# Reordering side work in a fused attention, feed-forward and gated-attention kernel on one core

## The reference

```python
def layernorm(x, gamma, beta):
    mean = jnp.mean(x, axis=-1, keepdims=True)
    std = jnp.sqrt(jnp.sum((x - mean) ** 2, axis=-1, keepdims=True) / (d - 1))
    return gamma * (x - mean) / (std + EPS) + beta

h = layernorm(x + multihead(x, x, x, sa_wq, sa_wk, sa_wv, sa_wo, causal=True), ln1_g, ln1_b)
h = layernorm(h + multihead(h, encoding, encoding, ca_wq, ca_wk, ca_wv, ca_wo, causal=False), ln2_g, ln2_b)
ff = jax.nn.relu(h @ ff_w1.T + ff_b1) @ ff_w2.T + ff_b2
x = layernorm(h + ff, ln3_g, ln3_b)
# gated attention, one head; q = x, k = v = context
qp, kp, vp = q @ Wq + bq, k @ Wk + bk, v @ Wv + bv
w = softmax(einsum('bqd,bkd->bqk', qp, kp) / sqrt(256))
y = einsum('bqk,bkd->bqd', w, vp)
gate = jnp.concatenate((qp, y), axis=-1) @ Wg + bg
out = y * mask * sigmoid(gate) + q
```

## Time and profile before

| what | value |
|---|---|
| median of 3 runs | 798.07 us (797.2 to 802.29) |
| the profiled execution | 799.49 us, its span 797.6 us |
| mean granted TensorE clock | 0.985 of full speed |
| PE, PEld busy | 753.8 us (94%), 620.5 us (78%) |
| DVE, ACT, POOL busy | 539.8 (68%), 526.0 (66%), 488.6 us (61%) |
| DMA | 77.05 MB, mean 97 GB/s |

### The profile page before, as it was taken

How to read it: one execution, slowest core, us unless ns; L and a number is a source line. 1 busy time by engine, 2 the same in 40 slices (tenths; PEclk the granted TensorE clock), 3 DMA queues, 4 the chain that set the end, 5 groups by cost and what they waited for, 6 DMA issues and landing times.

```text
span 797.6 us, 19831 instructions
## 1 busy us (share of the span) xinstructions
PE 753.8 (94%) x7136; PEld 620.5 (78%) x7136; DVE 539.8 (68%) x1202; ACT 526.0 (66%) x1241; POOL 488.6 (61%) x606
## 2 busy tenths in 40 slices
PE   6998999999999999788889999999999999999997
PEld 4786778878887776565568889888888879888875
DVE  4435778787887987876877666666666655575575
ACT  5432366566565566566878888888777888757663
POOL 3413377777677677767756666666565578665530
PEclk9998999999999999989989999999999999999999
DMA  9796697788765666435442222222220100012223
GB/s 287 173 278 178 132 148 133 144 133 137 136 123 108 112 108 125 105 86 119 88 83 57 39 57 57 59 56 55 56 47 6 61 2 5 10 51 65 64 79 102
DMA packets 105323, 77.05 MB, mean 97 GB/s; under 512 B 43277, under 2 KB 101983, under 8 KB 104963
## 3 DMA queue, kind: packets, MB, share of 16 engines
q1 hardware_dynamic: 101866, 72.89, 43.1%
q10 hardware_dynamic: 3360, 2.90, 1.2%
HBM read 25.75 MB, written 11.69 MB: 47 GB/s over the span
## 4 chain that ended last, share of the span: by engine, by line
PE 72%; DVE 7%; ACT 5%; issue 4%; POOL 1%; DMA 0%; ACTq 0%; DVEq 0%; POOLq 0%
PE a_misc L89 14%; PE a_pair L89 12%; PE a_s L1060 10%; PE a_pair L846 5%; PE a_s L822 4%; PE a_pair L864 4%; PE a_s L820 4%; PE a_pair L1019 4%; PE a_pair L1003 3%; PE a_pair L1159 3%; PE a_s L980 2%; PE a_s L1118 2%; DVE a_nm L1536 2%; PE a_pair L867 2%; ACT a_pT L1369 1%
## 5 line engine op out<-in xcount | busy, mean ns | idle before, releaser
L1227 ACT ACTIVATE a_pT<-a_pair 128x512 f32<-128x512 f32 x192 | 113.4, 597 | 76.8 <-PE a_pair L846 69.2
L2074 POOL TENSOR_TENSOR c_hidden<-c_hid,c_hidden 128x256 fp32r<-128x256 f32 x128 | 94.8, 741 | 108.4 <-ACT c_hidden L1403 108.2
L1536 DVE TENSOR_REDUCE a_nm<-a_s 128x2 f32<-128x512 f32 (+1 forms) x192 | 127.2, 677 | 50.2 <-PE a_s L822 49.4
L1060 PE MATMUL a_s<-c_w,c_hidden 128*128 128x256 f32 x768 | 117.1, 292 | 0.0
L1369 ACT ACTIVATE a_pT<-a_pair 77x512 f32<-77x512 f32 x128 | 75.1, 589 | 54.1 <-PE a_pair L1003 52.3
L89 PE MATMUL a_pair<-c_fxh,c_w 128*128 128x256 f32 x512 | 100.0, 288 | 1.5 <-ACT c_hid L1395 1.5
L1962 POOL TENSOR_SCALAR_AFFINE_SELECT a_pT<-a_pT 128x256 f32<-128x256 f32 (+1 forms) x192 | 89.2, 485 | 16.1 <-ACT a_pT L1227 16.0
L1060 PEld LDWEIGHTS a_s<-c_w,c_hidden 128*128 128x128 f32 x768 | 98.6, 190 | 0.4 <-issue 0.4
L1700 DVE TENSOR_REDUCE a_nm<-a_s 128x5 f32<-128x385 f32 (+1 forms) x96 | 55.4, 578 | 50.4 <-PE a_s L980 50.1
L89 PEld LDWEIGHTS a_pair<-c_fxh,c_w 128*128 128x128 f32 x512 | 79.3, 191 | 1.7 <-ACT c_hid L1395 1.7
L846 PE MATMUL a_pair<-a_sq,a_sk 98*128 98x256 bf16 (+1 forms) x512 | 75.3, 250 | 4.9 <-ACT a_pT L1227 4.7
(11 more groups left out here) (268 smaller groups left out, 2030.9 us busy)
## 6 DMA issues: line engine op xcount, KB each, us to landing
a_sq<-a_parts SPq DMA_DIRECT2D x96, 128.0 KB, 4.3
a_sk<-a_parts SPq DMA_DIRECT2D x96, 128.0 KB, 4.3
a_sq<-c_parts SPq DMA_DIRECT2D x96, 128.0 KB
x<-in_xT SPq DMA_DIRECT2D x16, 256.0 KB, 5.1
res<-in_x SPq DMA_DIRECT2D x16, 256.0 KB, 5.2
out<-g_fin SPq DMA_DIRECT2D x15, 256.0 KB, 2.1
a_sk<-kc_parts SPq DMA_DIRECT2D x96, 38.5 KB
g_vv<-vv_rows SPq DMA_DIRECT2D x16, 154.0 KB
```

Of the source, the lines that this page charges most:

```text
L1060: last = mt(down[:, qt * D:(qt + 1) * D], (hh, hl)[x](m)[:, qt * P:(qt + 1) * P], w2(y, m), start=m == 0 and qt == 0 and i == 0, stop=m == ...
L1227: nc.scalar.activation(pT[g % NPT][:], stps[g % 2][:], ACT.Exp).then_inc(s_exp, 1)
L1536: nc.vector.tensor_reduce(nm[c % 2][:, QT * heads[0] + qt:QT * heads[-1] + qt + 1:QT], sps[g % 2][:].rearrange("p (h k) -> p h k", h=len(h ...
L2074: nc.gpsimd.tensor_tensor(hl(m), hid[n % NHID][:], f32(hh(m)), ALU.subtract).then_inc(c_hl, 1)
```

## The change

It changes no arithmetic; it moves instructions and changes three semaphore waits.

- The context products use three banks, `kps[0]`, `kps[1]` and `tps[0]` (`key_ps`); product n waits for remainder n-3. `project_qk(0)`, which also writes `tps`, now waits for all six remainders.
- At n = 16 CROSS slot (0, 1) stands behind causal slot 2 instead of 1, so on every engine causal slot (16, 2), with the last causal shift, comes first.
- `first_deviations` of elements 8 to 11 goes from n = 16, slots 2, 5, 7 to n = 17, slots 8, 10, 11, in each ahead of what VectorE did there.
- At n = 15 the residual of element 12 comes ahead of `turn_av` instead of behind.
- Five pieces of feed weights are split one CROSS slot earlier on ScalarE (four on GpSimd).
- `cross_part_three` moves from slot 5, behind `cross_scale`, to slot 4, behind `shifted_rows2`, for every element.
- Group 8 to 11 of the third norm takes steps one and two in slots 4 and 6 of m = 18 instead of slots 2 and 3 of m = 19; step two of element 15 goes from CROSS (22, 6) to the end of GATED (12, 0).
- `normed(e + 3)` moves from GATED slot k = 3 to k = 1, and waits for `g_h` instead of `g_zg`.

```diff
@@ -150,6 +150,7 @@
     kps, tps, fps = [ps(f"k{i}") for i in range(2)], [ps(f"t{i}") for i in range(2)], [t.pair1[:, 512 * i:512 * (i + 1)] for i in range(2)]
     vps, vec = t.misc[:, 0:512], t.misc[:, 512:1024]
     qk_ps = lambda c: tps if c < 2 else kps
+    key_ps = lambda n: (kps + tps[0:1])[n % 3]
 
     w_loaded = {n: sem("xw_" + n) for n in raw}
     small, biases, c_loaded = sem("x_small"), sem("x_biases"), [sem("x_ctx") for _ in range(NC)]
@@ -245,15 +246,15 @@
                     pe.wait_ge(s_wl, 1)
                 if ot == 0:
                     pe.wait_ge(s_ch, c + 1)
-                atleast(pe, s_kr, n - 1)
+                atleast(pe, s_kr, n - 2)
                 for kt in range(KT):
                     for part in range(2):
-                        mt(kps[n % 2][:, 0:cn], cwk[part][:, kt, ot * P:(ot + 1) * P], ch[:, kt, c0:c0 + cn],
+                        mt(key_ps(n)[:, 0:cn], cwk[part][:, kt, ot * P:(ot + 1) * P], ch[:, kt, c0:c0 + cn],
                            start=kt == 0 and part == 0, stop=False, skip_group_check=True)
                 if ot == 0:
                     pe.wait_ge(s_cl, c + 1)
                 for kt in range(KT):
-                    last = mt(kps[n % 2][:, 0:cn], cwk[0][:, kt, ot * P:(ot + 1) * P], cl[:, kt, c0:c0 + cn],
+                    last = mt(key_ps(n)[:, 0:cn], cwk[0][:, kt, ot * P:(ot + 1) * P], cl[:, kt, c0:c0 + cn],
                               start=False, stop=kt == KT - 1, skip_group_check=True)
                 last.then_inc(s_k, 1)
 
@@ -272,6 +273,8 @@
 
             def project_qk(c):
                 pe.wait_ge(t.s_xl, c + 1)
+                if c == 0:
+                    pe.wait_ge(s_kr, KT * NC)
                 if c < 2:
                     atleast(pe, t.s_r1, 2 * c)
                 else:
@@ -364,7 +367,7 @@
                 ot, c = divmod(n, NC)
                 c0, cn = CCH[c]
                 act.wait_ge(s_k, n + 1)
-                nc.scalar.activation(parts[:, 0, c0 // SC:(c0 + cn) // SC, ot, :], byb(kps[n % 2], 0, cn), ACT.Copy).then_inc(s_kp1, 1)
+                nc.scalar.activation(parts[:, 0, c0 // SC:(c0 + cn) // SC, ot, :], byb(key_ps(n), 0, cn), ACT.Copy).then_inc(s_kp1, 1)
                 act.wait_ge(s_kr, n + 1)
                 nc.scalar.activation(parts[:, 1, c0 // SC:(c0 + cn) // SC, ot, :], byb(rest[n % 2], 0, cn), ACT.Copy).then_inc(s_kp2, 1)
                 if n in (2, 3):
@@ -427,7 +430,7 @@
                 c0, cn = CCH[c]
                 dve.wait_ge(s_kp1, n + 1)
                 atleast(dve, s_kp3, n - 1)
-                nc.vector.tensor_tensor(byb(rest[n % 2], 0, cn), byb(kps[n % 2], 0, cn), parts[:, 0, c0 // SC:(c0 + cn) // SC, ot, :],
+                nc.vector.tensor_tensor(byb(rest[n % 2], 0, cn), byb(key_ps(n), 0, cn), parts[:, 0, c0 // SC:(c0 + cn) // SC, ot, :],
                                         ALU.subtract).then_inc(s_kr, 1)
                 if n in (3, 4):
                     weight_low(n - 2)
@@ -579,8 +582,8 @@
     w2 = lambda a, m: w2_parts[a][m // 2][:, m % 2 * D:(m % 2 + 1) * D]
     pieces = [(raw_w[p // 2][:, p % 2], p // 2, w1_parts[0][p][:], w1_parts[1][p][:]) for p in range(4)]
     pieces += [(raw_w[2 + p // 2][:, p % 2], 2 + p // 2, w2_parts[0][p][:], w2_parts[1][p][:]) for p in range(4)]
-    piece_high = {(-1, 2): 0, (-1, 6): 1, (2, 1): 2, (2, 3): 3, (2, 5): 4, (3, 1): 5, (3, 3): 6, (4, 2): 7}
-    piece_low = {(-1, 3): 0, (-1, 7): 1, (2, 2): 2, (2, 4): 3, (2, 6): 4, (3, 2): 5, (3, 4): 6, (4, 3): 7}
+    piece_high = {(-1, 2): 0, (-1, 6): 1, (2, 0): 2, (2, 2): 3, (2, 4): 4, (3, 0): 5, (3, 2): 6, (4, 2): 7}
+    piece_low = {(-1, 3): 0, (-1, 7): 1, (2, 1): 2, (2, 3): 3, (2, 6): 4, (3, 1): 5, (3, 3): 6, (4, 3): 7}
     hid = [at(f"hid{i}", [P, S], F32, "a_o1", 4 * S * i) for i in range(2)] + [at("hid2", [P, S], F32, "a_on1")]
 
     s_ps, st_ps, av_ps, hy, qm, down = sps[0], stps[0], avps[0], bank0, bank1, sps[1]
@@ -652,7 +655,7 @@
     group_of = lambda c: next(i for i, r in enumerate(feed_groups) if c in r)
 
     beside = {B - 4: [-4], B - 3: [-3], B - 2: [-2], B - 1: [-1], B: [0], B + 1: [1], B + 2: [2, 3], B + 3: [4, 5]}
-    late = {B - 3: [0, 3, 6, 9, 11, 11, 11, 11], B: [0, 1, 3, 4, 6, 8, 11, 11],
+    late = {B - 3: [0, 3, 6, 9, 11, 11, 11, 11], B: [0, 2, 3, 4, 6, 8, 11, 11],
             B + 1: [0, 3, 6, 9, 9, 9, 11, 11]}
     order = []
     for n in range(-3, B + 4):
@@ -1439,7 +1442,7 @@
                 if c == 0:
                     stacks_dead(act, 0)
                 act.wait_ge(g_nmr, group_of(c) + 1)
-                atleast(act, g_zg, c - 1)
+                atleast(act, g_h, c - 1)
                 for qt in range(QT):
                     n = QT * c + qt
                     last = nc.scalar.activation(gz[c % 2][:, qt, :], t.res[:, n, :], ACT.Identity, scale=t.rstd[:, n:n + 1], bias=nmr[:, n:n + 1])
@@ -1511,6 +1514,7 @@
                     gated_x(e + 1)
                 if k == 3:
                     gated_x_high(e)
+                if k == 1:
                     normed(e + 3)
 
             for v in sk[1:]:
@@ -1627,17 +1631,20 @@
                     next_weight_low(s // 11)
                 if n == B - 4 and s in (0, 9, 10):
                     first_deviations(0, B // 2, (0, 9, 10).index(s))
-                if n == B and s in (2, 5, 7):
-                    first_deviations(B // 2, B - 4, (2, 5, 7).index(s))
+                if n == B + 1 and s in (8, 10, 11):
+                    first_deviations(B // 2, B - 4, (8, 10, 11).index(s))
                 if s == 5:
                     turn_av(n - 2, 0)
                 if s in (6, 7):
                     remainder(n + 2, s - 6)
                 if s == 8:
                     turn_back(n - 2, 0)
+                ahead = n == B - 1
+                if ahead and (n, s - 1) == out_slot(n - 3):
+                    residual(n - 3)
                 if s == 11:
                     turn_av(n - 2, 1)
-                if (n, s - 1) == out_slot(n - 3):
+                if not ahead and (n, s - 1) == out_slot(n - 3):
                     residual(n - 3)
 
             def centred2(c):
@@ -1683,10 +1690,10 @@
                     nc.vector.scalar_tensor_tensor(nmr[:, n:n1], t.mv[:, n:n1, 0], -1.0, t.rstd[:, n:n1], ALU.mult, ALU.mult).then_inc(g_nmr, 1)
 
             def deviation_slots(n, s):
-                group = n - 7 < feed_groups[2][-1] + 1
-                if s in (4, 6) and not group:
+                group = n - 7 < feed_groups[1][-1] + 1
+                if s in (4, 6) and not group and (n - 7, s) != (B - 1, 6):
                     yield n - 7, s // 2 - 1
-                if s in (2, 3) and n - 8 < feed_groups[2][-1] + 1:
+                if s in (2, 3) and n - 8 < feed_groups[1][-1] + 1:
                     yield n - 8, s - 1
 
             def cross_maxes(c, u):
@@ -1921,6 +1928,8 @@
                     shares(e)
                 if k == 0:
                     gated_x_low(e - 1)
+                if k == 0 and e == B - 4:
+                    feed_deviation(B - 1, 2)
 
             for stage, n, s in order:
                 if stage == CAUSAL:
@@ -2086,9 +2095,9 @@
                     cross_scale(n - 2, 0)
                 if s == 4:
                     shifted_rows2(n - 4)
+                    cross_part_three(n + 2)
                 if s == 5:
                     cross_scale(n - 2, 1)
-                    cross_part_three(n + 2)
                 if s == 6:
                     keep(n - 5)
                 if s == 7 and n > -4:
```

## The result

| | before | after |
|---|---|---|
| median of 22 runs each | 798.59 us (797.03 to 802.29) | 794.14 us (790.65 to 800.43) |
| the profiled execution | 799.49 us, span 797.6 | 794.01 us, span 792.1 |
| mean granted clock of it | 0.985 | 0.988 |
| PE busy / idle | 753.8 / 43.8 us | 751.1 / 41.0 us |

The ratio is 0.9941, with a 95% interval from 0.9921 to 0.9962: 0.6% faster, within the 1% that this text calls no change. The forecast was 789.4, with 784.5 to 796.0.

The account below looks back on a forecast made before the run. PE was taken to bound the kernel, busy 94% of the span, leaving only its 43.8 us idle and half-clock stretches to win. Terms summed to 8.7 us, taking the median from 798.07 to 789.4, range 784.5 to 796 (8 in 10).

Parts of the forecast that it names:

- third bank: At the start, PE waits less for VectorE's remainders and project_qk(0) moves from 24.15 to about 23.5: 0.6 us gain.
- residual, n = 15: Residual of element 12 ahead of turn_av; PE's wait of 0.94 us at 329.74 shrinks to 0.1: 0.8 us gain.
- shift ahead, and group leaves n = 16: In n = 16, PE's waits of 1.61 and 2.21 us for exponentials lose their cause: 3.2 us gain.
- group arrives in n = 17: Twelve small VectorE norm instructions in slots 8, 10, 11 delay residual 14, for which PE waits: 2.0 us loss.
- feed weights earlier: ScalarE's piece at 369.20 moves a slot earlier, shortening PE's wait of 1.16 us: 0.5 us gain; other pieces 0.
- third-norm shift earlier: ScalarE's shift leaves the way of PE's waits at 648.18 and 668.51, about 0.95 us each: 1.9 us gain.
- norm groups: Third-norm steps leave 696 to 702 us, where PE waits 1.27 us for the shares: 1.2 us gain.
- half clock: The 5.9 us half-clock stretch after 340.7 goes once the 2.21 us wait goes: 2.5 us gain.
- Two signs named there: No PE wait over 0.6 us between 330 and 341 for residual or exponentials; PE idle down about 6 us.
- what would make me wrong: Idle time falls but the span does not, or PE's waits from 340 to 400 grow by what 330 to 340 lost.
- first rival: Chance 0.20: the 5.9 us half-clock stretch stays, or the new wait in n = 17 brings another; 791.9 us.
- second rival: Chance 0.19: idle time moves on between engines from 330 to 400; terms 3.2, 2.5, 1.9 halve; 793.2 to 795.1, middle 794.

Follow-up runs that it names:

- bank_only: Kernel before with only the third bank for the context products and the wait for all six remainders: -0.30 (0.46) us against before at equal clock.
- res_back: Changed kernel with the residual of element 12 behind turn_av again (n = 15): +0.52 (0.50) us at equal clock.
- shift_only: Kernel before with only CROSS slot (0, 1) moved behind causal slot 2 of n = 16: -0.69 (0.46) us against before at equal clock.
- norm16: Changed kernel with the norm group of elements 8 to 11 back in n = 16, slots 2, 5, 7: -0.55 (0.61) us at equal clock.
- low_back: Changed kernel with GpSimd's low half of feed weight piece 3 one slot later, in CROSS (2, 4): -1.29 (0.65) us at equal clock.
- k3: Changed kernel with ScalarE's third-norm shift and scale back in GATED slot 3, still waiting for g_h: +1.74 (0.50) us at equal clock.
- norm_gap: Changed kernel with the norm group of elements 8 to 11 in n = 17, slots 2, 3, 10: -1.96 (0.65) us at equal clock.
- after_again: Changed kernel profiled again, no edit; five PE waits the same to 0.01 us, half clock at other places; no separate time given.
- best1: Changed kernel with norm group in slots 2, 3, 10, piece 3 at (2, 4), normed in slot 1 only for e < 7: median 789.03 us.
- best2: best1 with the residual ahead of the turn in n = 16 to 18 too: median 787.82 us, -0.35 (0.95) us against best1.
- before_again: Kernel before profiled again, no edit; waits the same to 0.01 us but for the 1.16 us; no separate time given.

## Why the forecast was right in kind and 4.7 us too low

| term of the sum | forecast | by the runs | from |
|---|---|---|---|
| third bank | 0.6 | 0.85 (times: 0.3) | both traces, bank_only |
| residual, n = 15 | 0.8 | 0.75 | traces, res_back |
| shift ahead, and group leaves n = 16 | 3.2 | 0.7 + 1.2 = 1.9 (first pair of traces: 2.3) | shift_only, norm16 |
| group arrives in n = 17 | -2.0 | -1.4 to -2.0 | norm16; two waits, 0.96 and 1.00 |
| feed weights earlier | 0.5 | 0.5 - 1.3 = -0.8 | traces, low_back |
| third-norm shift earlier | 1.9 | 1.97 - 0.9 = 1.1 (times: 1.7) | traces, k3 |
| norm groups | 1.2 | 1.47 | traces |
| sum without clock | 6.2 | 3.45 | times at equal clock |
| half clock | 2.5 | 1.1 | below |
| sum | 8.7 | 4.45 | medians |

The terms measured one by one add up to 3.6 us, with the arrival at 1.7. Each is uncertain by some tenths, and traces and times differ by more than that for the shift, the third bank and the third-norm shift; within that nothing large is missing.

**Right.** The start, the residual, the cost of the arrival (the group took 3.25 us where I counted 3.6, and L993's wait is 1.56, foretold as 1 to 2.5), the three waits at 648, 668 and 703, the full clock from 330 to 350, and 23.30 for 23.5. Within 1% had the largest chance, 0.49. Two signs named there failed: a wait of 0.77 us was left between 330 and 341, where I allowed 0.6, and PE's idle time fell by 2.8 us instead of 6. That the gain of 330 to 340 is partly given back between 340 and 400 was named as what would make me wrong, and it did.

**Wrong, first: shift and group were added up.** I let the 1.61 and the 2.21 us both vanish, one by the shift, one by the group's leaving. But norm16 and shift_only show that the first edit already undoes most of the second cause: with the shift in time the group starts before GpSimd's addition and takes 3.9 us instead of 5.46; of the waits of 1.61 and 2.21 us 0.77 and 1.13 are left, and the 0.77 is there in the changed kernel too. Leaving n = 16 is then worth 1.2 us, by the shift between norm16's and the changed kernel's traces from 330 to 343 us, and coming to n = 17 costs 1.4 by the same two traces up to 367: the move as a whole lost 0.2 us by the traces and 0.55 (0.61) by the times, which is not to be told from nothing. The step that failed is the one that took both durations of the group from the trace of before and let them stand after an edit in front of it.

**Wrong, second: `weight_low` costed at nothing.** I wrote that the pieces stand where GpSimd waits for its input. For piece 3 that is so only when GpSimd is not late; here it had a weight piece, a norm addition and a second piece in a row from 361.23 to 365.19, with PE's input behind them. I had a bound of 0.6 for a select that is pushed back; what was pushed back was L1988, with 1.27 us of L2073 in front.

**Wrong, third: the late price of the third-norm shift.** I named what ScalarE was free of, and not what GpSimd would do with an input that comes two slots earlier: its two operations move onto VectorE's product. The Trainium skill, page "SBUF — State Buffer", section "Who interferes with whom", says that such a VectorE instruction, with two inputs in SBUF, contends with GpSimd's reads and that the first issued keeps the port. The trace agrees (1.32 us instead of 0.48, ended 0.3 us behind GpSimd's). I had weighed this rule for n = 17 alone.

**The clock.** The step itself, no half clock near 340 once the 2.21 us wait is gone, holds in all profiles: the three profiles with that wait (before twice, bank_only) have 6.8 us of it there, the ten without have none between 306 and 359. But half clock is not won for good. Of those ten, five show it between 359 and 384 us, where before has none, for 10.2, 3.4, 6.8, 13.7 and, in two pieces, 13.6 us (after, low_back, norm16, norm_gap, k3); shift_only, after_again and res_back have none there, the two mended ones 3.4 us from 382. Seven of the ten have one or both of the new waits of 1.4 to 1.6 us (for the residual and for L1988), and the five are among them. In each of these the clock fell during such a wait or at most 2.0 us behind its end; the three with neither wait (shift_only, best1, best2) show no fall there. So a new wait belongs to the fall as far as thirteen profiles can tell, but does not bring it each time. As a mean over runs, twice the missing clock times the span gives 21 us at half clock for before, 17.6 for after and 13 for the mended kernel. The 1.2 to 4.1 us behind the last matmul are in all three. At its own place the term was well sized: the same matmuls took 5.85 us in before and 3.22 in after, 2.63 won (the prediction halved 5.9 to 2.95 and took 2.5 for waiting; in fact the work takes more than half of its time at full clock). Of the 6.8 us that go at 340, about half come back elsewhere; 0.0022 of clock at 5.0 us for 0.01 is 1.1 us. This is my first rival (the new wait brings another stretch), in part of the executions. The second rival gave the size, 794, but not by halving what it named, so that its number fits is luck.

**Open.** What makes the clock fall in one execution and not in the next at the same waits was not found: at 73 us it did in six of thirteen profiles. No run had the feed weights on both engines back, and before_again shows the wait of 1.16 us that they were to shorten split in two with no time lost or won, so that the 0.5 us are ScalarE's piece is read from the traces and not shown. The norm groups of the third norm and `cross_part_three` were not taken back alone either: the 1.47 us, more than the bound of 1.27, are the shift of the traces at that place. What the shift alone wins lies between 0.69 (0.46) us by the times and 1.4 by the traces.

## What to carry to other kernels

A duration that was stretched by a neighbour belongs to a place and not to an instruction: after an edit in front of it, count it anew before adding the next edit's gain. For each instruction that is made earlier, ask both what it stands in front of in its own queue and which engine its result wakes earlier, and what that one then collides with. Free time in a queue (2.06 us in one piece here) is a better home for a group of small instructions than a slot that is merely less critical: the same twelve took 5.46, 3.25 and 1.97 us.
